# Layer 1's score products in a two-layer graph attention kernel: from plain fp32 to three short products of split operands

## The reference, cut to what matters

```python
# layer 0
scores = einsum('bihd,bjhd->bhij', Q, K) / sqrt(hd)
soul_bias = a[:, :, None] + c[:, None, :] + b_g
scores = scores + (soul_bias + log(adjacency + EPS))[:, None, :, :]
x = einsum('bhij,bjhd->bihd', softmax(scores), V).reshape(B, N, D) + x
# layer 1
q = x @ Wq + bq;  k = x @ Wk + bk
scores = einsum('bod,bid->boi', q, k) / sqrt(512)
attn = where(mask, 0.0, softmax(where(mask, -1e18, scores)))
ctx = einsum('boi,bie->boe', attn, x) @ Wc
out = layernorm(x + ctx) * gamma + beta
```

## Time and profile before

| what | value |
|---|---|
| time, median of 3 runs | 2290.16 us (2290.14 to 2292.62) |
| profiled execution, its own time | 2289.82 us |
| its span, first to last instruction | 2288.0 us |
| PE, PEld busy | 2250.0 us (98%), 1875.8 us (82%) |
| DVE, ACT, POOL busy | 1839.3 us (80%), 1219.3 us (53%), 989.3 us (43%) |
| mean granted clock of TensorE, as a share of 2.4 GHz | 0.992 |

### The profile page before, as it was taken

The page is one execution under the profiler, slowest core; times in us unless marked ns, Lnnn a source line. Parts: engine busy times, 40 slices in busy tenths (PEclk is TensorE's granted clock), DMA queues, the critical chain, the costliest instruction groups (busy, mean ns, idle before and its releaser), DMA issues.

```text
span 2288.0 us, 39399 instructions
## 1 busy us (share of the span) xinstructions
PE 2250.0 (98%) x13284; PEld 1875.8 (82%) x13284; DVE 1839.3 (80%) x5508; ACT 1219.3 (53%) x3474; POOL 989.3 (43%) x1146
## 2 busy tenths in 40 slices
PE   9999999999999999999999999999999999999986
PEld 6888888888888888888888888888888888888864
DVE  5678888878788888888888888788788787878776
ACT  5555555655555555455555455555556555555542
POOL 0244344454354453445443445543444543544422
PEclk9999999999999999999999999999999999999997
DMA  7333334333333333333333343333333333333321
GB/s 240 111 128 108 125 115 136 126 113 125 114 126 126 130 107 125 120 130 120 130 111 127 111 137 125 129 107 124 117 135 129 114 122 115 125 124 131 102 80 41
DMA packets 187305, 277.98 MB, mean 121 GB/s; under 512 B 24672, under 2 KB 122592, under 8 KB 182880
## 3 DMA queue, kind: packets, MB, share of 16 engines
q1 hardware_dynamic: 186528, 274.42, 36.2%
q10 hardware_dynamic: 576, 1.05, 0.1%
HBM read 166.54 MB, written 108.86 MB: 120 GB/s over the span
## 4 chain that ended last, share of the span: by engine, by line
PE 89%; DVE 4%; DMA 2%; POOL 2%; SPq 1%; issue 1%; ACT 1%; DVEq 0%; POOLq 0%
PE bank L223 25%; PE bank L225 25%; PE bank L224 25%; PE bank L467 5%; PE bank L503 5%; PE bank L480 5%; DVE x1n L1040 1%; POOL x1n L1296 0%; POOL probs L1265 0%; POOL x1n L1291 0%; DMA probsT<-turn_dram 0%; DMA gamma_b<-in_gamma 0%; DMA turn_dram<-turned 0%; ACT probs L742 0%; DMA out<-x1n 0%
## 5 line engine op out<-in xcount | busy, mean ns | idle before, releaser
L1265 POOL TENSOR_TENSOR probs<-probs,rcp 128x512 f32<-128x512 f32 x256 | 291.4, 1153 | 900.8 <-DVE rcp L980 900.8
L742 ACT ACTIVATE probs<-probs,nmax 128x128 f32<-128x128 f32 x1024 | 397.5, 390 | 177.2 <-DVE nmax L970 176.5
L1040 DVE STREAM_TRANSPOSE x1n<-x1T 32x512 f32<-32x512 f32 x512 | 359.9, 703 | 41.3 <-DMA out<-x1n 33.6
L1273 POOL TENSOR_TENSOR x_lo<-xT_land,x_hi 128x512 fp32r<-128x512 f32 x124 | 168.1, 1387 | 328.6 <-ACT x_hi L698 328.6
L970 DVE CUSTOM_DVE_ANT_0 probs<-bank,bias 128x128 f32<-128x128 f32 x1024 | 228.4, 286 | 5.6 <-issue 2.8
L223 PE MATMUL bank<-x_hi,wm_hi 128*128 128x512 f32 x512 | 205.5, 401 | 9.4 <-DVE x_lo L1002 9.4
L223 PE MATMUL bank<-x_hi,wk_hi 128*128 128x512 f32 x512 | 204.6, 400 | 3.6 <-DVE x_lo L913 3.0
L726 ACT ACTIVATE k_sb<-bank,cols 128x512 f32<-128x512 f32 x128 | 88.3, 690 | 223.3 <-PE bank L225 223.1
L223 PE MATMUL bank<-wc_hi,x_hi 128*128 128x512 f32 x512 | 203.9, 398 | 0.0
L223 PE MATMUL bank<-wv_hi,x_hi 128*128 128x512 f32 x512 | 203.1, 397 | 0.0
L763 ACT ACTIVATE g_sb<-bank,consts 128x512 f32<-128x512 f32 x128 | 87.5, 684 | 212.8 <-PE bank L225 211.0
(11 more groups left out here) (132 smaller groups left out, 5341.9 us busy)
## 6 DMA issues: line engine op xcount, KB each, us to landing
turn_dram<-turned SPq DMA_DIRECT2D x128, 512.0 KB, 2.6
probsT<-turn_dram SPq DMA_DIRECT2D x512, 128.0 KB, 2.6
out<-x1n SPq DMA_DIRECT2D x128, 256.0 KB, 2.0
xn<-in_x SPq DMA_DIRECT2D x126, 256.0 KB, 3.3
xT_land<-in_xT SPq DMA_DIRECT2D x31, 1024.0 KB, 6.9
adj_sb<-in_adj SPq DMA_DIRECT2D x32, 256.0 KB, 3.1
c_rows<-c_dram SPq DMA_DIRECT2D x32, 256.0 KB, 3.2
at_dram<-scratch SPq DMA_DIRECT2D x31, 256.0 KB, 2.0
```

Source lines behind the costliest of these rows:

```text
L742: op = nc.scalar.activation(probs[:, k, :], probs[:, k, :], ACT.Exp, bias=nmax[:, k:k + 1], scale=-1.0, accum_out=sums[:, k:k + 1])
L1040: op = nc.vector.transpose(x1n[b * BLK:(b + 1) * BLK, :, :] .rearrange("p g (c a s) -> p a c g s", c=C, a=P // BLK)[:, a, :, :, :], x1T[a ...
L1265: nc.gpsimd.tensor_tensor(probs[:, half, :], probs[:, half, :], rcp[:, half].unsqueeze(2).to_broadcast([P, HALF, P]), ALU.mult)\
L1273: nc.gpsimd.tensor_tensor(x_lo[:, c, :], xT_land[(t + 1) % 2][:, c, :], x_hi[:, c, :].bitcast(f32), ALU.subtract).then_inc(s["pool_x"], 1)
```

## The change

- `pair_scores` takes split operands: the high part of G (`g_hi`, what ScalarE's copy now writes, type f32r), a low part `g_lo`, and the high and low parts of x1, which already exist. For each chunk and graph there are three short products of 128 columns instead of one fp32 product.
- `g_lo` is made by VectorE in a new function `g_low`: bank plus bias minus `g_hi`, 128x512. There is one buffer, so chunk c waits until `pair_scores` c - 1 is over. Four calls stand in VectorE's step.
- `pair_scores` waits for `g_low` (`dve_g`), no longer for `g_out`. Waits for `act_g` further on, now implied, are gone.
- The fourth score product moves behind `project_k(t, 2)`.
- The bias of layer 0 is written over the logarithm (`ln_adj`); the tile `bias0` is gone. The next logarithm waits for the last maxima of the step before, no longer for the bias.
- Two landing places of a weight load at the start become `v1_b` and `adj_sb[1]`, and the load of the second adjacency moves behind the first step's moves of probabilities.

```diff
             def pair_scores(u, c, last):
-                pe.wait_ge(s["act_g"], nth("act_g", u, c))
+                pe.wait_ge(s["dve_g"], nth("dve_g", u, c))
                 for g in range(GG):
                     cols_g = slice(g * P, (g + 1) * P)
-                    mm = nc.tensor.matmul(sa_bank(last)[:, cols_g], g_sb[c % 2][:, cols_g],
-                                          x1T[:, c, cols_g], start=(c == 0 and g == 0),
-                                          stop=(c == C - 1), skip_group_check=True)
+                    pairs = ((g_hi[c % 2], x1_hi), (g_hi[c % 2], x1_lo), (g_lo, x1_hi))
+                    for i in range(3):
+                        mm = nc.tensor.matmul(sa_bank(last)[:, cols_g], pairs[i][0][:, cols_g],
+                                              pairs[i][1][:, c, cols_g], start=(c == 0 and g == 0 and i == 0),
+                                              stop=(c == C - 1 and i == 2), skip_group_check=True)
                 mm.then_inc(s["pe_sa"], 1)
...
                 gw(3)
                 pair_scores(u, 2, False)
+                project_k(t, 2)
                 pair_scores(u, 3, False)
-                project_k(t, 2)
                 project_q(t, 2)
-                pe.wait_ge(s["act_g"], nth("act_g", u, 2))
                 project_k(t, 3)
-                pe.wait_ge(s["act_g"], nth("act_g", u, 3))
                 project_q(t, 3)
...
-                    op = nc.vector.scalar_tensor_tensor(out=bias0[:, g, :], in0=c_row[:, g, :],
+                    op = nc.vector.scalar_tensor_tensor(out=ln_adj[:, g, :], in0=c_row[:, g, :],
...
+            def g_low(u, c, last):
+                dve.wait_ge(s["act_g"], nth("act_g", u, c))
+                if c > 0:
+                    dve.wait_ge(s["pe_sa"], nth("pe_sa", u, c - 1))
+                nc.vector.scalar_tensor_tensor(out=g_lo[:, :], in0=g_bank(c, last)[:, :],
+                                               scalar=u1_c[:, c:c + 1], in1=g_hi[c % 2][:, :].bitcast(f32),
+                                               op0=ALU.add, op1=ALU.subtract).then_inc(s["dve_g"], 1)
...
             def this_log_adj(it):
-                act.wait_ge(s["dve_b"], nth("dve_b", it.t - 1))
+                act.wait_ge(s["dve_max"], nth("dve_max", it.t - 1, 2 * C - 1))
                 log_adj(it.t, it.p + 1, it.par)
...
                 x1lo(u, 3)
-                for a in range(P // BLK):
+                for a in range(2):
+                    x1_rows(u, a)
+                for c in range(C):
+                    g_low(u, c, True)
+                for a in range(2, P // BLK):
                     x1_rows(u, a)
...
                 recips(t, 0)
+                g_low(u, 0, False)
                 x1_rows(u, 1)
+                g_low(u, 1, False)
                 turn(t, 0)
                 maxima(t, 1)
+                g_low(u, 2, False)
                 x1_rows(u, 2)
+                g_low(u, 3, False)
                 x1_rows(u, 3)
                 recips(t, 1)
```

More of the change, by code:

```diff
@@ L88, in gnn_program @@
         x1_lo = sb("x1_lo", [P, C, COLS], f32r)
-        g_sb = [sb(f"g_sb{i}", [P, COLS]) for i in range(2)]
+        g_hi = [sb(f"g_hi{i}", [P, COLS], f32r) for i in range(2)]
+        g_lo = sb("g_lo", [P, COLS], f32r)
         y_hi = [sb(f"y_hi{i}", [P, D], f32r) for i in range(2)]
@@ L98, in gnn_program @@
         c_rows = sb("c_rows", [P, P * GG])
-        bias0 = sb("bias0", [P, GG, P])
         mask = sb("mask", [P, GG, P], bf16)
@@ L106, in gnn_program @@
         beta_b = sb("beta_b", [P, D])
-        wq1_land = [g_sb[0][:, :], g_sb[1][:, :], flat(att1), beta_b[:, :]]
         wg1_b = sb("wg1_b", [P, D])
@@ L111, in gnn_program @@
         v1_b = sb("v1_b", [P, D])
+        wq1_land = [v1_b[:, :], flat(adj_sb[1]), flat(att1), beta_b[:, :]]
         ident = sb("ident", [P, P])
@@ L132, in gnn_program @@
         bank = [ctx.enter_context(nc.psum_tensor(f"bank{i}", [P, 512], f32)) for i in range(8)]
-        PER = dict(pe_q=4, pe_k=4, pe_s=8, pe_v=4, pe_pv=4, pe_g=4, pe_sa=4,
+        PER = dict(pe_q=4, pe_k=4, pe_s=8, pe_v=4, pe_pv=4, pe_g=4, pe_sa=4, dve_g=4,
                    pe_y=4, pe_tp=1, pe_ctx=4,
@@ L356, in body @@
                     load_xT(t + 1, 1 - it.par)
-                    load_adj(t + 1, 1 - it.par)
                 if w >= 0:
@@ L380, in body @@
                         sp.wait_ge(s_m, C + 1)
+                        load_adj(t + 1, 1 - it.par)
                         sp.dma_start(beta_b[:, :], beta.to_broadcast([P, D])).then_inc(s_beta, 16)
@@ L551, in layer1_alone @@
                 for y in range(2, GG):
-                    pe.wait_ge(s["act_g"], nth("act_g", u, y - 2))
                     if y == GG - 1:
-                        pe.wait_ge(s["act_g"], nth("act_g", u, 3))
                         turn_attention(u)
@@ L762, in g_out @@
                     act.wait_ge(s["pe_sa"], nth("pe_sa", u, c - 2))
-                nc.scalar.activation(g_sb[c % 2][:, :], g_bank(c, last)[:, :], ACT.Identity,
+                nc.scalar.activation(g_hi[c % 2][:, :], g_bank(c, last)[:, :], ACT.Identity,
                                      bias=u1_c[:, c:c + 1]).then_inc(s["act_g"], 1)
@@ L971, in maxima @@
                             out=probs[:, k, :], in0=s_banks(c)[h][:, (k % HALF) * P:(k % HALF + 1) * P],
-                            in1=bias0[:, k % HALF, :], scale=1.0, scalar=BIG, op0=ALU.add, op1=ALU.min,
+                            in1=ln_adj[:, k % HALF, :], scale=1.0, scalar=BIG, op0=ALU.add, op1=ALU.min,
                             accum_out=nmax[:, k:k + 1])
```

## The result

The changed kernel takes 2563.9 us (median of 4 runs, 2555.8 to 2575.0), against 2291.4 us for the kernel before in the same comparison: a ratio of 1.119, with a 95% interval from 1.114 to 1.124. The forecast was 2483 us with a range to 2545. The direction was right; the slowdown was 273 us where 193 were forecast, and the time lies outside the range.

The account below looks back on a forecast made before the run. TensorE, busy for all of a full step, was taken to bound the kernel. 31 steps x 6.0 = 186 us of lateness and 7.3 in the closing part, on 2289.8, gave 2483 us, range 2405 to 2545.

Parts of the forecast that it names:

- TensorE bounds the kernel, and the price of a product is its load: TensorE is busy throughout the full steps; a short score product costs its weight load, 0.112 us.
- the dear and the cheap rival: Short score products at 0.227 us each, 2543 us, chance 0.08; or at 0.057 with hidden load, 2264 us, chance 0.05.
- VectorE's chain to `turn(t, 1)`: In each step, 2.7 us of `g_low` work and 5.2 us of two waits on VectorE make `turn(t, 1)` 8.0 us late.
- That the price of the products is inside the waits: Between 0.057 and some 0.13 us, TensorE's price of a short product changes nothing in the 6.0 us a step.
- What TensorE is late at the scores: 6.0: In each step `pv(t, 1)` starts 6.0 us later: `turn(t, 1)` is 8.0 late against 2.0 of slack.
- That also gives 6.0, so nothing is added.: Layer 1's turned attention: 8.0 us late, less 1.0 got back and 1.0 of slack, so no extra cost.
- The clock: At TensorE's new waits in each step the forecast charged no loss of clock.
- The forecast wait of 3.3 us is shorter than what was borne: TensorE had idled 3.7 us with full clock granted; the wait at `pv(t, 1)` is shorter, against a clock fall.
- The rival itself: The clock falls to 1.2 GHz in the new waits: 1.5 us a step, 46 us on top, 2530 us, chance 0.09.
- The closing part: Behind the steps VectorE is the path; low parts and score blocks alternate on one `g_lo` buffer: 7.3 us late.

Follow-up runs that it names:

- fp32 run: The changed kernel with the fp32 score products of before, `g_lo` still made and waited for but not used: 2545.4 us, ratio 1.111.

## Why the prediction was wrong

- *TensorE bounds the kernel, and the price of a product is its load.* Right: 0.112 forecast, 0.114 measured, and the dear and the cheap rival fall.
- *VectorE's chain to `turn(t, 1)`.* Right step by step: 8.3 us late, forecast 8.0. A `g_low` takes 751 ns; I had taken 0.68 from the earlier trace rows, which scales by a constant, where the earlier trace rows, with a scalar for each partition as here, had 1.62 for two. Four times 0.07 is the 0.3.
- *That the price of the products is inside the waits.* Right but for 8 to 19 of some 60 us, by the fp32 run, and the 8 come from the clock.
- *What TensorE is late at the scores: 6.0.* Measured 6.45, as VectorE was 0.3 later and some transfers landed late (the wait was up to 4.5 us).
- *"That also gives 6.0, so nothing is added."* Too small. I had the lateness of the turned attention and its slack from one step, each to about 1 us, found them equal and took the equality for cover. They cost 0.75 us a step in full clock. This and the term above make 1.2 us a step, 37 us.
- *The clock.* This is the step that failed. "The forecast wait of 3.3 us is shorter than what was borne", from the earlier trace rows: 3.7 us of idling at full clock before the closing part. The sum had the loss of clock at nothing; it was 37 us. With waits of 2.8 to 4.5 us the clock fell in 29 of 31 steps, in the step shown some 2 us after TensorE had gone idle. One stretch that was borne is no bound. The rival itself was right, at a chance of 0.09 and with 1.5 us a step where 1.2 were measured. That the sizes are so near is in part luck: its 1.5 us were read from seven products at the kernel's start, 3.1 us at half clock, while here the half clock lasted 3.4 or 6.8 us and part of its cost took the place of another wait. Behind the wait stand `pv(t, 1)` and the scores 2 and 3, 3 us at full clock; in the step shown all of it runs at half clock, in others a part.
- *The closing part.* 7.3 forecast. From the last first score block to the end it is 45.6 us against 38.9: 6.7.

The terms add up: 2483 + 37 + 37 = 2557, the profiled execution. Either of the two misses alone would have left the time inside the range.

## What to carry to other kernels

Price a short f32r product by its stationary operand, not by its columns: splitting pays where one load serves many moving columns, and with 128 of them three loads cost more than the two passes of fp32 that they replace (0.34 against 0.22 us). With 512 the three cost 0.68 us, and the two passes of fp32 would cost 0.86, by four such passes at the start of the kernel before, which start 0.43 apart:

```profile
35.07 1.88 PE L405 MATMUL bank<-x1n,g_sb 128*128 128x512 f32 x4
36.79 1.02 PE L405 MATMUL bank<-x1n,att 128*128 128x512 f32 x2
```

Where between them it turns was not measured.

When a new instruction goes into the queue of a second engine, count its waits and not its length, follow every result behind it to TensorE, and compare each lateness with its slack; where the two come out equal, charge for it. A wait of 2 to 3 us on TensorE in every step should be priced with the half clock behind it, unless rows show that such waits are borne each time; the waits of 1 us for `g_lo` never let the clock fall here.

## What the runs showed of the hardware that I had not expected

The clock fell after about 2 us of idling in one place and not within 3.7 us in another of the kernel before. In the same place of 31 like steps it fell between 1.9 and 4.5 us after TensorE had gone idle, and twice not at all. Waits of 1.95 us were followed by a fall in 13 of 31 steps of the fp32 run, waits of 2.8 to 4.5 us in 29 of 31 of the kernel after. So from such rows one can tell how often a wait is borne, not a length up to which it is. And more work made the kernel faster: unused products in the wait gave back 37 us.
